# The last attention of a transformer stack on one core: four blocks turned into one block that works tile by tile

## The reference

```python
def _dyn_quant(x):
    s = jnp.maximum(jnp.max(jnp.abs(x), axis=-1, keepdims=True) / 127.0, EPS)
    q = jnp.clip(jnp.round(x / s), -127.0, 127.0)
    return (q, s)
...
def _w8a8_linear(x, w, b):
    qx, sx = _dyn_quant(x)
    qw, sw = _quant_weight(w)
    y = jnp.einsum('bnc,oc->bno', qx, qw) * (sx * sw[:, 0])
    return y + b
...
q = _w8a8_linear(x, wq, bq).reshape(B, N, H, D).transpose(0, 2, 1, 3)
k = (cond @ wk.T + bk).reshape(B, L, H, D).transpose(0, 2, 1, 3)
v = (cond @ wv.T + bv).reshape(B, L, H, D).transpose(0, 2, 1, 3)
scores = jnp.einsum('bhnd,bhld->bhnl', q, k) * inv_sqrt_d + mask[:, None]
attn = jax.nn.softmax(scores, axis=-1)
o = jnp.einsum('bhnl,bhld->bhnd', attn, v)
o = o.transpose(0, 2, 1, 3).reshape(B, N, C)
return _w8a8_linear(o, wo, bo)
...
x = x + _L3_xattn_ref(_layernorm(x, axis=-1), ctx_2048, mask_BxSxS2_ff0, ...)
```

## Time and profile before

| what | value |
|---|---|
| median of 3 runs | 1227.47 us (1227.47, 1227.47, 1230.66) |
| profiled execution, its own time | 1230.68 us |
| its span, first to last instruction | 1228.9 us |
| c1, from the first key product to the barrier | 871.5 to 904.3 |
| c2 | 904.4 to 915.1 |
| c3 | 915.4 to 972.7 |
| c4 | 973.0 to 981.0 |
| first instructions of the last mixture | 981.3 |

### The profile page before, as it was taken

The page is one execution under the profiler, slowest core; times in us unless marked ns, Lnnn a source line. Parts: engine busy times, 40 slices in busy tenths (PEclk is TensorE's granted clock), DMA queues, the critical chain, the costliest instruction groups (busy, mean ns, idle before and its releaser), DMA issues. The chain is left out here.

```text
span 1228.9 us, 20831 instructions
## 1 busy us (share of the span) xinstructions
PE 1073.5 (87%) x6796; PEld 761.8 (62%) x6799; DVE 913.5 (74%) x1737; ACT 780.6 (64%) x1228; POOL 546.6 (44%) x736
## 2 busy tenths in 40 slices
PE   4888956699889978999789999999777688999998
PEld 3545523444568855555668888888434476888886
DVE  5667887624767767888877777777758877777777
ACT  5567867489557745777456777666554455767774
POOL 7243547003536603126436666664120156666662
PEclk8788967799999988999989999999879799999999
DMA  6763120477224316432134453332010011433342
GB/s 180 223 191 104 42 81 1 111 203 198 69 76 129 110 31 187 137 112 71 32 101 126 124 192 121 121 123 75 23 27 1 7 33 42 123 119 119 119 119 73
DMA packets 74143, 125.21 MB, mean 102 GB/s; under 512 B 10401, under 2 KB 43873, under 8 KB 73431
## 3 DMA queue, kind: packets, MB, share of 16 engines
q1 hardware_dynamic: 72342, 117.87, 32.9%
q0 software_dynamic: 864, 6.03, 1.4%
q10 hardware_dynamic: 864, 0.39, 0.1%
HBM read 108.21 MB, written 15.45 MB: 101 GB/s over the span
## 5 line engine op out<-in xcount | busy, mean ns | idle before, releaser
L2130 POOL TENSOR_TENSOR f_up_lo<-f_w_up,f_up_hi 128x1024 fp32r<-128x1024 f32 (+1 forms) x70 | 164.7, 2352 | 162.3 <-ACT f_up_hi L1980 162.3
L1135 ACT ACTIVATE a_probs<-a_p_sc 128x1024 f32<-128x1024 f32 x192 | 189.4, 1019 | 29.0 <-PE a_p_sc L1007 21.6
L1279 DVE TENSOR_REDUCE a_maxes<-a_p_max 128x2 f32<-128x512 f32 x256 | 160.1, 682 | 50.4 <-PE a_p_max L974 50.0
L1007 PE MATMUL a_p_sc<-a_q,a_k 75*128 75x256 bf16 (+1 forms) x768 | 118.9, 282 | 11.4 <-DMA a_q<-a_neg_t 6.4
L1812 PE MATMUL f_p_y<-f_hid_hi,f_down_hi 128*128 128x512 f32 x304 | 120.9, 398 | 4.1 <-DVE f_hid_lo L2284 1.9
L1812 PE MATMUL f_p_y<-f_hid_lo,f_down_hi 128*128 128x512 f32 x304 | 119.7, 394 | 0.0
L1812 PE MATMUL f_p_y<-f_hid_hi,f_down_lo 128*128 128x512 f32 x304 | 119.3, 392 | 0.0
L1028 PE MATMUL a_p_out<-a_probs,all_v 128*32 128x256 f32 x1536 | 111.8, 402 | 0.3 <-ACT p_out L1143 0.3
L1007 PEld LDWEIGHTS a_p_sc<-a_q,a_k 75*128 75x128 bf16 (+1 forms) x768 | 68.9, 100 | 60.0 <-ACT a_probs L1135 21.7
L2249 DVE TENSOR_TENSOR f_p_u<-f_p_u,p_x_t 128x512 f32<-128x512 f32 x67 | 46.9, 699 | 79.0 <-PE f_p_u L1798 78.9
L974 PE MATMUL a_p_max<-a_k,a_q 72*128 72x256 bf16 x512 | 91.4, 292 | 15.2 <-DMA a_q<-q_parts 8.4
(11 more groups left out here) (411 smaller groups left out, 2765.5 us busy)
## 6 DMA issues: line engine op xcount, KB each, us to landing
f_coef<-coef SPq DMA_DIRECT2D x43, 512.0 KB, 3.6
f_w_up<-in_w SPq DMA_DIRECT2D x70, 256.0 KB, 3.0
a_q<-q_parts SPq DMA_DIRECT2D x48, 288.0 KB
f_w_down<-in_w SPq DMA_DIRECT2D x76, 128.0 KB, 2.0
a_k<-k_plain SPq DMA_DIRECT2D x96, 96.0 KB
a_k<-k_unit SPq DMA_DIRECT2D x24, 192.0 KB
outs<-p_out SPq DMA_DIRECT2D x32, 128.0 KB, 1.9
p_whole<-outs SPq DMA_DIRECT2D x32, 128.0 KB, 2.6
```

The source lines that it names most:

```text
L1007: last = nc.tensor.matmul(p_sc[pair % 2][:, h % 2, t * D:(t + 1) * D], k_of(b, h, K_ROWS)[:, t * P:(t + 1) * P], q_of(b, h, K_ROWS), start ...
L1135: nc.scalar.activation(probs[b % 2][:, 2 * pair:2 * pair + 2, :, :].rearrange("p h t d -> p h (t d)"), p_sc[pair % 2][:], ACT.Exp, scale=s ...
L1279: nc.vector.tensor_reduce(maxes[b % 3][:, :, h], p_max[:, n % 3, :].rearrange("p (t d) -> p t d", t=NK), axis=AX.X, op=ALU.max, negate=Tru ...
L2130: nc.gpsimd.tensor_tensor(up_lo[slot(t, 2)][:, 0:width], w_up[slot(t, 2)][:, 0:width], up_hi[slot(t, 2)][:, 0:width], ALU.subtract).then_i ...
```

## The change

The four blocks become one, without a barrier inside.

- The weights' scales are measured at the end of the mixture ahead (`measure_weights`, VectorE, behind its last `low`).
- The keys are kept for two heads at a time (`k_pairs`): 8 copies on ScalarE. The selection among the pairs moves to the query: `copy_q` makes four copies of 128x128 a tile, with scale and bias from tiles, where c3 had one of 128x256. `scores` is 16 products of 64 rows by 64 columns and 128 moving columns, in place of 4 of 128 by 64 and 512. A query is scaled by the weights' scales and biased in `copy_q`, by the tokens' scales in `scale_q`.
- The value products take their bias as a third product (a column of the identity against `bias_v`), go four batches to a bank, and are copied by ScalarE (`copy_values`). They stand in two rows of eight batches, one behind the keys and one between `turn_q(1)` and `turn_x(2)`.
- Six of the eight norms are applied by ScalarE (`apply_by_act`).
- From then on each engine has one loop over tiles, in which projection of tile i+3, scores of i+2, probabilities of i+1 and output of i-1 follow each other. The residual additions are all on VectorE; GpSimd adds the output's bias. The router's and the first weights' loads are issued at the start of the block.

```diff
+                def measure_weights():
+                    dve.wait_ge(m.raw_loaded, 32)
+                    for n in range(2):
+                        last = nc.vector.tensor_reduce(m.w_largest[:, n, :], m.raw[n][:], axis=AX.X, op=ALU.max,
+                                                       apply_absolute_value=True)
+                    link(last)
+                    link(nc.vector.tensor_scalar(m.w_deq[:], m.w_largest[:], 1.0 / 127.0, 1e-8, ALU.mult, ALU.max))
+                    nc.vector.reciprocal(m.w_factor[:], m.w_deq[:]).then_inc(m.scale_ready, 1)
...
+                if layer == 2:
+                    measure_weights()
                 dve.wait_ge(y_done, 2)
...
+        p_k = [p_s[0], p_s[1], p_p[0], p_p[1]]
...
+                def values(b):
...
+                    for odd in range(2):
+                        for k in range(NK):
+                            nc.tensor.matmul(bank[64 * odd:64 * odd + 64, at:at + P], cond[:, k, b * L:(b + 1) * L],
+                                             wv[:, k, :].rearrange("p (q s c) -> p q s c", s=2, c=XC)[:, :, odd, :],
+                                             start=(k == 0), stop=False)
+                        last = nc.tensor.matmul(bank[64 * odd:64 * odd + 64, at:at + P], bc(m.ident[:, 0:1], [0, L]),
+                                                bias_v[:].rearrange("p (q s c) -> p q s c", s=2, c=XC)[:, :, odd, :],
+                                                start=False, stop=True)
+                    if b % VALUES == VALUES - 1:
...
+                        for j in range(2):
+                            for r in range(2):
+                                rows = slice(64 * r, 64 * r + 64)
+                                for b2 in range(2):
+                                    last = nc.tensor.matmul(
+                                        p_s[r][64 * b2:64 * b2 + 64, (2 * k + j) * P:(2 * k + j + 1) * P],
+                                        q_t[i % 2][rows, k, j, 64 * b2:64 * b2 + 64],
+                                        k_pairs[rows, k, 2 * i + b2, :, :].rearrange("p h l -> p (h l)"),
+                                        start=True, stop=True)
+                    last.then_inc(s_done, 1)
...
+                pe.wait_ge(m.cond_loaded, 3 * 16)
+                for g in range(4):
+                    keys(g)
+                for n in range(4):
+                    two_values(n)
+                turn_weights(0)
+                turn_x(0)
+                queries(0)
+                turn_q(0)
+                turn_x(1)
+                queries(1)
+                scores(0)
+                turn_q(1)
+                for n in range(4, 8):
+                    two_values(n)
+                turn_x(2)
+                queries(2)
+                scores(1)
+                turn_q(2)
+                turn_probs(0)
+                weigh(0)
+                turn_weights(1)
+                for i in range(NI + 1):
+                    if i + 3 < NI:
+                        turn_x(i + 3)
+                        queries(i + 3)
+                    if i + 2 < NI:
+                        scores(i + 2)
+                    if i + 3 < NI:
+                        turn_q(i + 3)
+                    if i + 1 < NI:
+                        turn_probs(i + 1)
+                        weigh(i + 1)
+                    if i >= 1:
+                        turn_o(i - 1)
+                        outputs(i - 1)
+
+            @block.scalar
...
+                def copy_keys(g):
+                    n, k2 = g // 2, g % 2
+                    act.wait_ge(k_done, g + 1)
+                    for h in range(2):
+                        copy(k_pairs[:, k2, 8 * n:8 * n + 8, h, :], p_k[g][:].rearrange("p (b l) -> p b l", l=L),
+                             ACT.Identity, bias=bk_own[:, k2, h:h + 1], scale=own[:, h:h + 1]).then_inc(k_copied, 1)
...
+                        act.wait_ge(s_done, i - 1)
+                    for k in range(NK):
+                        for j in range(2):
+                            last = copy(q_t[i % 2][:, k, j, :], p_q[:, D + k * P:D + (k + 1) * P], ACT.Identity,
+                                        bias=bq_own[:, k, j:j + 1], scale=w_own[:, k, j:j + 1])
...
+                copy_keys(0)
+                whole_weights(0)
+                copy_keys(1)
+                act.wait_ge(norm.shift_ready, 1)
+                for i in range(BY_VECTOR, NI):
+                    norm.apply_by_act(i)
+                whole_x(0)
+                copy_weights(0)
+                copy_x(0)
+                copy_keys(2)
+                scale_q(0)
+                whole_x(1)
...
+                whole_x(3)
+                exps(0)
+                copy_probs(0)
+                whole_weights(1)
+                copy_weights(1)
+                for i in range(NI + 1):
+                    if i + 3 < NI:
+                        copy_x(i + 3)
+                        scale_q(i + 3)
+                        copy_q(i + 3)
+                    if i + 1 < NI:
+                        exps(i + 1)
+                        copy_probs(i + 1)
+                    if i >= 1:
+                        whole_o(i - 1)
+                        copy_o(i - 1)
+                    if i + 4 < NI:
+                        whole_x(i + 4)
+                    if i in (3, 4):
+                        front.split_high(act, lambda out, src: copy(out, src, ACT.Copy), i - 3)
+
+            @block.vector
+            def _(dve):
...
+                for i in range(NI + 2):
+                    if i + 1 < NI:
+                        soften(i + 1)
+                    if i + 4 < NI:
+                        quantize_x(i + 4)
+                    if 1 <= i <= NI:
+                        quantize_o(i - 1)
+                    if i < NI:
                         divide(i)
-                    quantize(NI - 1)
-
-
-        with ExitStack() as ctx:
```

More of the change, by code:

```diff
@@ L54, in align @@
         if gap:
-            self.sb("gap", [P, gap // 4])
+            self.sb(f"gap{self.nc.sbuf_base}", [P, gap // 4])
     def over(self, name, shape, dt, at):
@@ L430, in place_last_attention @@
     m.cond = part(4 * NK * D, T)
+    m.w_largest, m.w_deq, m.w_factor = [part(4 * NK * D + NK * T + 4 * n, 2) for n in range(3)]
 def load_last_attention(sp, m, a):
@@ L2977, in token_scale @@
     link(nc.vector.reciprocal(factor, deq))
+BY_VECTOR = 2
+VALUES = 4
 def quantized_attention(nc, m, a, front):
[L2982 to L3382 removed]
@@ L3415, in program @@
         m.cond_loaded = st.sem("cond_loaded")
+        m.scale_ready = st.sem("scale_ready")
         early = ExitStack()
@@ L3520, in layout @@
     arrays["xk_w"], arrays["xv_w"] = width_first(I["L3_xattn_wk"].T), width_first(I["L3_xattn_wv"].T)
-    arrays["xq_b"], arrays["xo_b"], arrays["xv_b"] = I["L3_xattn_bq"], I["L3_xattn_bo"], I["L3_xattn_bv"]
-    arrays["xk_b"] = I["L3_xattn_bk"].reshape(NK, P).T
-    arrays["own"] = (p[:, None] // XC == np.arange(8)[None]).astype(f)
+    arrays["xo_b"], arrays["xv_b"] = I["L3_xattn_bo"], I["L3_xattn_bv"]
+    arrays["xk_b"], arrays["xq_b"] = I["L3_xattn_bk"].reshape(NK, P).T, I["L3_xattn_bq"].reshape(NK, P).T
+    of_head = np.stack([p // XC % 2 == 0, p // XC % 2 == 1, p // (2 * XC) % 2 == 0, p // (2 * XC) % 2 == 1], 1)
+    arrays["own"] = of_head.astype(f)
     arrays["cond"] = width_first(ctx.reshape(T, D).T)
```

719 lines of the change are left out of this document (370 added, 349 removed).

## The result

The changed kernel takes 1244.57 us (median of 1241.36, 1244.12, 1245.02 and 1246.2) where the kernel before takes 1227.47 (1225.57 to 1230.66). The ratio is 1.0133, with a 95% interval of 1.0104 to 1.0163: slower by 1.3%. The forecast was 1240, in a range of 1220 to 1255.

What follows compares the result with a forecast made beforehand. The prediction took the kernel as one chain of stages, the new loop as a closed circle of TensorE and ScalarE. Terms -0.7 + 11.3 + 1.0 = +11.6 us gave 1239.1 on the median, written 1240, range 1220 to 1255.

Steps and rivals of the forecast that it cites:

- Front part: From first key product to the end of the first exponentials: ends at 912.1, 13.1 us earlier than before.
- `copy_q` 1.6: ScalarE's four query copies per tile, .38 us each, 1.6 with the end; bounds .9 and 2.1.
- Rival 3: Value products run in series, 1.5 for .7 us a batch: up to +12 us, forecast 1251; chance .08.
- `measure_weights` at 0: Four added VectorE instructions ahead of the region fill idle time: 0 us, bounds 0 and 1.9.
- The turn at full clock: One loop turn over tiles, a closed circle of TensorE and ScalarE, takes 9.9 us.
- Scores: 16 products, 32 records per turn: 1.3 us taken, between 1.13 (four quarters side by side) and 1.95 (column halves only).
- the .25 for hand-overs: Part of each loop turn: .25 us for hand-overs between engines not contained in the listed durations.
- rival 4: Shorter loop turn, 9.0 us, with `copy_q` at .9 and scores at 1.13: -6.7 us at full clock, 1221; chance .18.
- The clock: TensorE's waits in the loop lower its clock: 2.8 us a turn, 22.5 over eight turns, half taken: +11.3 us.
- rival 2: Clock at the lower level in the whole loop: +23.8 us, forecast 1251; chance .12.
- L: Stretch from the end of the first exponentials to the next stage's first filler: 68.2 and .3 us, plus 11.3 for the clock.
- Hand-over: The next stage's 32 filler products, 3.65 us before, could start at the lower clock: +1.0 us.

Runs made afterwards that it cites:

- e1_fill12: Changed kernel plus 12 idle products of 256 columns in each of five turns, between the query transpose and the probability transposes; 1236.52 us, ratio 1.0034 to the kernel before.
- e7_fill_first: Changed kernel plus 30 idle products of 256 columns only in TensorE's wait for the first exponentials; 1245.0 us, ratio 1.0086 to the kernel before.
- e2_exps_first: Changed kernel with ScalarE's exponentials, probability copies and output rounding put ahead of the query copies in each turn; 1225.63 us, ratio 0.9947 to the kernel before.
- e5_both: Changed kernel with exponentials ahead of query copies and four value batches moved into TensorE's waits between first projections; 1226.29 us, ratio 0.9941 to the kernel before.
- e6_early_exps: Changed kernel with exponentials ahead of query copies, four value batches strewn into waits, and first exponentials moved behind tile 1's query copies; 1213.19 us, ratio 0.9843 to the kernel before.

## Why the prediction was right, and where it erred

The direction and the size hold: 1240 against 1244.57. The reason for the slowdown, a circle of TensorE and ScalarE in which a wait brings the clock down, holds too. But that the number came so near is partly luck: the turn at full clock and the clock's cost were both mis-sized, and the two errors cancelled.

- **Front part.** I had 40.6 us from the first key product to the end of the first exponentials; it was 39.9. The pieces hold too: rows of 5.6 us were 5.7, `copy_q` 1.6 was 1.51. Rival 3 (products in series) is out: 96 records take 5.7 us, .06 each. One reading there was wrong, though no sum used it: the old value row of 13.20 us holds 96 of 128 records, 12 of the 16 batches, so the new products save more than I said.
- **`measure_weights` at 0.** It holds. From the last `f_hid_lo` to the copy of `f_p_y` are 863.89 to 866.33 before and 859.44 to 861.88 after, 2.44 us both times, with the new reductions inside:

```profile
859.44 0.69 DVE L2285 TENSOR_TENSOR f_hid_lo<-f_p_g,f_hid_hi 128x512 fp32r<-128x512 f32 x1 [0.67 <-ACT f_hid_hi L2028]
860.05 1.27 DVE L2345 TENSOR_REDUCE all_v<-all_v 128x2 f32<-128x512 f32 x2
...
861.88 0.69 DVE L2482 COPY f_y_t<-f_p_y 128x512 f32<-128x512 f32 x1
```

- **The turn at full clock: mis-sized, 9.9 for 9.15 (e1_fill12).** The circle is the right one. Scores take 1.03 us to the next instruction where I took 1.3: the term was at the lower end, near the 1.13 of another 32 records in the weighing; had only the column halves worked together, it would have been 1.95. The Trainium skill ("TensorEngine Tiling (Array Packing)", Tiling Modes) lists 64x64 as a mode of four tiles. The 1.03 agrees with four at work. From `copy_q` to the exponentials behind it are 1.39 us (948.22 to 949.61) where I took 1.6, and the .25 for hand-overs was already in the durations. The other steps were off by up to .14 either way, and come to nothing. So rival 4's turn of 9.0 was nearly true, but for another reason than its price of .9 for `copy_q`.
- **The clock: mis-sized.** A turn loses 3.3 us at the lower clock, where I had 2.8. What was missing is the transposes of the probabilities: from their start to the weighing are 2.74 us at 0.50 (941.56 to 944.30) and 1.93 at 1.00, .8 for my .28, because both of ScalarE's copies then wait for TensorE. And I took half of the turns as low; the windows show 0.64 to 0.67 up to 932 and 0.50 in all of 932 to 972. That is rival 2 more than the forecast. My reason for the half, that a slower TensorE is busier and so gets the clock back, didn't happen: it was busy for 6 to 7.7 of 10 us and stayed low.
- **The sum.** For L I had 68.5 (68.2 and .3) + 11.3 = 79.8, and 82.4 came. Five turns .75 too long hid part of a clock loss that was too small: from the end of `exps(0)` to the end of `exps(5)` were 59.5 us, where my 48.6 and the clock's 11.3 make 59.9. The tail from the end of `exps(5)` (966.42) to 989.30 was 22.9 for 19.6, in part at 0.50, and that is where L missed.
- **Hand-over.** The next stage's 32 fillers took 5.04 us for 3.65, +1.4 for my +1.0.
- **The picture to expect.** `exps(0)` ended 39.9 us behind the first key product, the turns were 10.4 to 12.5 apart, TensorE's wait ahead of the transposes was released by ScalarE's exponentials. The granted clock of 0.50 was below the 0.6 to 0.9 that I had named.

What I didn't see in the trace of before is how cheap the remedy is. The prediction named the place (`exps(i+1)` behind `copy_q(i+3)`), and took the order as given.

## What to carry to other kernels

When stages are merged into one pipelined loop, write the turn down as a circle: each engine's list in order, and each wait between them. If the sum of the circle exceeds every engine's busy time, look for a step whose input is long ready (here the exponentials, behind copies two tiles ahead) and move it up: here that gave 2.4 us a turn, and with TensorE's idle piece gone the clock's 3.3 as well. Products that have slack belong into the waits, where here they cost nothing and kept the clock; the same products as a row cost their length.

## What the runs showed of the hardware

- An idle piece of 2.54 us in a turn of 12.46 went with a clock of 0.50 for 40 us on end, though TensorE was busy for 62 to 77% of it; with 12 fillers in the turn and 1.23 us of idle time, the clock was at 1.00 for 30 us (e1_fill12, 922 to 952) and at 0.53 in the next 10. No run tells what in the turn decides it.
- 30 fillers (3.44 us, granted clock 1.00) followed by 2.44 us of idle time didn't keep the clock for what came behind: the transposes took 1.97 us (e7_fill_first).
- 32 records of 64 rows by 64 columns with 128 moving columns take 1.10 us at 1.00 (e1_fill12) and 1.99 at 0.50 (the changed kernel).
- The first eight records of key products, the same code behind the same idle time of 3.23 us, took 6.4 to 6.6 us in most profiles and 3.7 in three of them (e2_exps_first, e5_both, e6_early_exps). The granted clock of their first half was 0.50 in the changed kernel (867.0 to 870.3) and 1.00 in e6_early_exps (870.85 to 872.7). So 2.9 us of a single execution hang on the clock at this place, apart from any edit.
